# Identity matmul of a key block moved next to its score matmuls in the attention loop of a fused macaron layer

## What is computed

```python
Q = (hidden_states @ Wq.T).reshape(B_, T_, H, D)          # H = 16 heads, D = 128
latent_k = hidden_states @ Wk.T                           # L = 64
latent_v = hidden_states @ Wv.T
q_latent = jnp.einsum('bthd,hdl->bthl', Q, q_to_latent)
logits = jnp.einsum('bthl,bsl->bhts', q_latent, latent_k) * inv_sqrt_L
causal = j <= i
logits = jnp.where(causal[None, None], logits, NEG)
band = (jnp.abs(i - j) <= RA_WINDOW) & causal             # RA_WINDOW = 64
logits = jnp.where(band[None, None], logits + RA_ALPHA * logits_recip, logits)
attn = jax.nn.softmax(logits, axis=-1)
V_exp = jnp.einsum('btl,hld->bthd', latent_v, v_up)
ctx = jnp.einsum('bhts,bshd->bthd', attn, V_exp)
out = ctx.reshape(B_, T_, H * D) @ Wo.T
```

## Time and profile before

| | us |
|---|---|
| median of 3 runs | 3462.59 |
| lowest and highest run | 3459.32, 3469.61 |
| the profiled execution's own time | 3459.25 |
| its span (first to last instruction, slowest core, core 4) | 3457.7 |
| spans of the 8 cores | 3441.6 to 3457.7 |

### The profile page before, as it was taken

How to read it: one execution, slowest core, us unless ns; L and a number is a source line. 1 busy time by engine, 2 the same in 40 slices (tenths; PEclk the granted TensorE clock), 3 DMA queues, 4 the chain that set the end, 5 groups by cost and what they waited for, 6 DMA issues and landing times.

```text
span 3457.7 us, 31678 instructions; the slowest of 8 cores (3441.6 to 3457.7 us)
## 1 busy us (share of the span) xinstructions
PE 2826.7 (82%) x10542; PEld 1005.4 (29%) x10719; DVE 1118.0 (32%) x2081; ACT 696.7 (20%) x1149; POOL 51.4 (1%) x78
## 2 busy tenths in 40 slices
PE   4988669866986698679288888888888888888797
PEld 1333124312432243233022222222222222233333
DVE  2003220332023202411344454555545555411203
ACT  2110211022102210200033333333333333302010
POOL 0000000000000000000000000000000000000000
PEclk8997789888988898889555565565556555689898
DMA  5420233123411341041100000000000000050442
GB/s 134 69 49 0 100 60 65 22 100 49 73 25 73 76 73 25 0 76 34 21 1 1 1 1 1 1 1 1 1 1 1 1 1 1 4 95 0 73 73 98
DMA packets 15218, 128.16 MB, mean 37 GB/s; under 512 B 6417, under 2 KB 6730, under 8 KB 7610
## 3 DMA queue, kind: packets, MB, share of 16 engines
q0 software_dynamic: 6848, 82.28, 14.0%
q1 hardware_dynamic: 8218, 43.83, 3.5%
HBM read 196.53 MB, written 9.27 MB: 60 GB/s over the span
## 4 chain that ended last, share of the span: by engine, by line
PE 76%; DVE 12%; issue 4%; ACT 3%; DMA 3%; DVEq 0%; POOL 0%; ACTq 0%; SPq 0%; POOLq 0%
PE bp_p L318 23%; PE PB L1466 7%; PE PD L1469 7%; PE PC L1390 6%; DVE xhat L242 5%; PE fe_p L573 4%; PE fe_p L515 4%; PE ln_sum L183 4%; PE ln_sum L186 4%; PE PC L1425 3%; PE PA L1255 2%; PE PA L1304 2%; PE bp_p L331 1%; PE bp_cs L288 1%; ACT probs L1447 1%
## 5 line engine op out<-in xcount | busy, mean ns | idle before, releaser
L318 PE MATMUL bp_p<-xhat,wslotP 128*128 128x512 bf16 x2503 | 565.1, 383 | 63.7 <-DVE xhat L242 57.5
L1447 ACT ACTIVATE probs<-PC 128x512 bf16<-128x512 f32 (+3 forms) x768 | 352.7, 486 | 783.6 <-PE PC L1425 483.5
L1466 PE MATMUL PB<-probs,ones_bf 128*1 128x512 bf16 (+3 forms) x768 | 343.4, 447 | 20.2 <-ACT probs L1447 19.3
L318 PEld LDWEIGHTS bp_p<-xhat,wslotP 128*128 128x128 bf16 x2560 | 245.9, 99 | 383.2 <-issue 104.4
L1390 PE MATMUL PC<-qlat_h,kaug 65*128 65x256 bf16 (+3 forms) x1088 | 328.5, 400 | 30.4 <-ACT probs L1447 19.5
L1469 PE MATMUL PD<-probs,vexp 128*128 128x512 bf16 (+3 forms) x705 | 323.9, 459 | 0.0
L176 ACT ACTIVATE ln_sq<-x_res 128x1024 bf16<-128x1024 f32 x144 | 152.1, 1056 | 742.5 <-DVE x_res L583 329.0
L1408 DVE COPY_PREDICATED mr<-bandm_sb,ob 128x256 bf16<-128x256 uint8 (+1 forms) x512 | 210.6, 411 | 111.6 <-DVE ob L1348 63.9
L1425 PE MATMUL PC<-mr,ident_bf 128*128 128x256 bf16 (+1 forms) x576 | 185.2, 343 | 66.0 <-DVE mr L1408 63.5
L358 ACT ACTIVATE bbuf<-bp_p,b_sb 128x1024 bf16<-128x1024 f32 x80 | 89.1, 1114 | 673.7 <-PE bp_p L331 673.7
L242 DVE TENSOR_TENSOR xhat<-x_res,ln_rrep 128x1024 bf16<-128x1024 f32 x144 | 163.6, 1211 | 24.2 <-PE ln_rrep L232 24.2
(11 more groups left out here) (167 smaller groups left out, 2110.4 us busy)
## 6 DMA issues: line engine op xcount, KB each, us to landing
x_res<-xall SPq DMA_DIRECT2D x16, 2048.0 KB, 7.7
wslotP<-w1q POOLq DMA_DIRECT2D x16, 2048.0 KB, 15.1
wslotP<-varr POOLq DMA_DIRECT2D x4, 2048.0 KB, 14.8
wslotP<-uarr POOLq DMA_DIRECT2D x4, 2048.0 KB, 14.8
wslotP<-wqq POOLq DMA_DIRECT2D x4, 2048.0 KB, 15.5
wslotF<-woq POOLq DMA_DIRECT2D x4, 2048.0 KB, 15.7
wslotF<-w1q POOLq DMA_DIRECT2D x4, 2048.0 KB, 15.6
yout<-x_res SPq DMA_DIRECT2D x4, 2048.0 KB
```

The costliest lines, as they stand in the source:

```text
L318: mi = t.matmul(P[par][:, 512 * half:512 * half + 512], lhsT, rhs_sb[:, NTOK * k + 512 * half: NTOK * k + 512 * half + 512], start=(k == 0 ...
L1447: s.activation(probs[i % 2][:, a:b], PC[:, a + dlt:b + dlt], AF.Exp).then_inc(cs.h, 1)
L1466: t.matmul(PB[:, a:b], bufs['ones_bf'][:, 0:1], probs[i % 2][:, a:b], start=(i == 0), stop=last)
```

## The change

Three of the TensorE helpers (scores, imm, sums_ctx) become one, `emit_iter`, which issues in turn `i` sums_ctx of block i-2, scores of block i and then, directly behind them, imm of block i. Before, imm of block i was issued at the head of turn i+1, behind that turn's stage of `emit_A_stage` or epilogue part. exp of block i is now issued at the end of turn i, and so on ScalarE ahead of what the stages and the epilogue of turn i+1 issue; before it stood behind them. outer(i) and select(i) stay where they were on VectorE: behind the turn's stage and epilogue part. No instruction is added or taken away, and no tile, width, DMA or wait condition is changed.

```diff
-                    def emit_scores(i, first_waits):
-                    def emit_imm(i):
-                    def emit_sums_ctx(i):
...
+                    def emit_iter(i, first_waits):
+                        fw = tuple(first_waits)
                         @block.tensor
...
+                            if i >= 2:
+                                j = i - 2
...
+                                for (a, b) in split_ranges(qlo, NTOK, (512,)):
+                                    t.wait_ge(cs.h,
+                                              exp_toks[j][(a + dlt) // 512])
...
+                            if i < NT:
...
+                                    mi = t.matmul(
+                                        PC[:, a + dlt:b + dlt],
+                                        kaug[0:65, 128 * i:128 * i + 128],
+                                        ql[0:65, a:b],
+                                        start=first, stop=stop)
+                                mi.then_inc(ct.h, 1)
+                                sco_toks[i] = ct.inc()
+                            if i < NT:
...
+                                t.wait_ge(cv.h, mr_toks[i])
...
+                                    mi = t.matmul(
+                                        PC[:, a + dlt:b + dlt],
+                                        bufs['ident_bf'][:, :],
+                                        mr_sb[i % 4][:, a - qlo:b - qlo],
+                                        start=False, stop=True)
+                                mi.then_inc(ct.h, 1)
+                                imm_toks[i] = ct.inc()
...
-                        if 1 <= i <= NT:
-                            emit_imm(i - 1)
                         if i < NT:
                             emit_outer(i)
-                        if 1 <= i <= NT:
-                            emit_exp(i - 1)
-                        if i >= 2:
-                            emit_sums_ctx(i - 2)
+                            emit_select(i)
+                        fw = [(dsy.h, st['r64']), PF['pc']] if i == 0 else []
+                        emit_iter(i, fw)
                         if i < NT:
-                            fw = [(dsy.h, st['r64']), PF['pc']] if i == 0 \
-                                else []
-                            emit_scores(i, fw)
-                            emit_select(i)
+                            emit_exp(i)
```

More of the change, by code:

```diff
@@ L1451, in emit_exp, with _ @@
                         exp_toks[i] = toks
-                    def emit_sums_ctx(i):
-                        qlo = qlo_of(i)
+                    def emit_iter(i, first_waits):
+                        fw = tuple(first_waits)
                         @block.tensor
-                        def _(t, i=i, qlo=qlo, st=st, vex=vex,
+                        def _(t, i=i, fw=fw, st=st, vex=vex, ql=ql,
                               pbf=PF['pb'], pdf=PF['pd']):
[L1458 to L1474, removed]
@@ new lines, in _ @@
+                            if i >= 2:
+                                j = i - 2
+                                qlo = qlo_of(j)
+                                dlt = pc_delta(j)
+                                if j == 0:
+                                    t.wait_ge(cv.h, st['ve7'])
+                                    t.wait_ge(pbf[0], pbf[1])
+                                    t.wait_ge(pdf[0], pdf[1])
+                                for (a, b) in split_ranges(qlo, NTOK, (512,)):
+                                    t.wait_ge(cs.h,
+                                              exp_toks[j][(a + dlt) // 512])
+                                    last = (j == NT - 1
+                                            or qlo_of(j + 1) >= b)
+                                    t.matmul(PB[:, a:b],
+                                             bufs['ones_bf'][:, 0:1],
+                                             probs[j % 2][:, a:b],
+                                             start=(j == 0), stop=last)
+                                    mi = t.matmul(
+                                        PD[:, a:b],
+                                        vex[:, 128 * j:128 * j + 128],
+                                        probs[j % 2][:, a:b],
+                                        start=(j == 0), stop=last)
+                                mi.then_inc(ct.h, 1)
+                                sc_toks[j] = ct.inc()
@@ new lines, in _ @@
+                            if i < NT:
+                                qlo = qlo_of(i)
+                                lead = min(256, NTOK - qlo)
+                                dlt = pc_delta(i)
+                                for sem, val in fw:
+                                    t.wait_ge(sem, val)
+                                seen_banks = set()
+                                if dlt == 0:
+                                    pieces = split_ranges(
+                                        qlo, NTOK, (qlo + lead, 512))
+                                else:
+                                    pieces = split_ranges(
+                                        qlo, NTOK, (qlo + lead,))
+                                lead_banks = {(qlo + dlt) // 512,
+                                              (qlo + lead - 1 + dlt) // 512}
+                                pieces.sort(
+                                    key=lambda p: ((p[0] + dlt) // 512
+                                                   in lead_banks, p[0]))
+                                for (a, b) in pieces:
+                                    bank = (a + dlt) // 512
+                                    first = bank not in seen_banks
+                                    if first:
+                                        for back in (1, 2):
+                                            pe = exp_toks.get(i - back)
+                                            if pe is not None and bank in pe:
+                                                t.wait_ge(cs.h, pe[bank])
+                                                break
+                                    seen_banks.add(bank)
+                                    last_in_bank = (b + dlt ==
+                                                    min(512 * (bank + 1),
+                                                        NTOK + dlt))
+                                    stop = (last_in_bank
+                                            and bank not in lead_banks)
+                                    mi = t.matmul(
[5 more added lines that the diff above has]
+                                sco_toks[i] = ct.inc()
@@ new lines, in _ @@
+                            if i < NT:
+                                qlo = qlo_of(i)
+                                lead = min(256, NTOK - qlo)
+                                dlt = pc_delta(i)
+                                t.wait_ge(cv.h, mr_toks[i])
+                                cuts = (512,) if dlt == 0 else ()
+                                for (a, b) in split_ranges(qlo, qlo + lead,
+                                                           cuts):
+                                    mi = t.matmul(
+                                        PC[:, a + dlt:b + dlt],
+                                        bufs['ident_bf'][:, :],
+                                        mr_sb[i % 4][:, a - qlo:b - qlo],
+                                        start=False, stop=True)
+                                mi.then_inc(ct.h, 1)
+                                imm_toks[i] = ct.inc()
```

## The result

The changed kernel takes 3548.32 us (median of 10 runs) against 3461.3 for the kernel before (10 runs): slower by 2.56%, ratio 1.0256 with a 95% interval of 1.0217 to 1.0296. The forecast was 3560 in a range of 3530 to 3595, so time and direction came as predicted. Some executions of every kernel ran with one die's cores at a lower clock; ratios leave them out, and where only two others were left for a variant, both times are given in place of a ratio.

What follows compares the result with a forecast made beforehand. TensorE was taken to set the pace in attention, mostly at 1.2 GHz. Wait terms, chiefly +83.4 us for the loop in turns 26 to 31, summed to +98.7 us on 3459.25, put at 3560 us, range 3530 to 3595.

Steps and rivals of the forecast that it cites:

- TensorE's pace and the closed loop: Attention: TensorE sets the pace; stage matmuls, evacuation, outer, select, imm close a loop of 2.67 or 2.39 us a turn.
- the loop's term: Turns 26 to 31: 14.90 us against 9.48, +5.42; with imm shifts +5.56 a head, +83.4 us over 15 heads.
- Turns 1 and 2: Head start: later rep and stage 0 behind imm(1), +20.0 and +0.5 us; stage 0's long evacuations, +4.5 us.
- Turns 3 to 15: Stages 10 and 11 +3.0 us, stage 12 later +5.0, exponential wait of 0.59 gone -8.9, over 15 heads.
- Turns 22 to 25: Exponential wait of 0.75 us goes, block 24's selection delayed 0.2: -0.55 in 16 heads, -8.8 us.
- The clock: TensorE's granted clock over 15 heads: unknown size, 42 us more to 50 less, taken as 0.
- the sum of 98.7: Whole kernel: all wait terms added, +98.7 us over the kernel before.
- The colder rival: Attention: added waits also take away the 2.4 GHz stretches, 42 us more, 3602 us; chance 0.09.
- the rule of the Trainium skill: TensorE: slow clock is default, recent activity releases it, so added waits cost clock, towards 42 us more.
- The faster rival: Attention: stage matmuls fill TensorE's 34.9 us of waits for exponentials and VectorE keeps up, 3428 us; chance 0.06.

Runs made afterwards that it cites:

- 0.98: Kernel before, with imm and exp of the previous block moved ahead of the stage in turns 4 and 22 alone; ratio 0.9817.
- An edit that removed a wait: Changed kernel with outer and select first in every turn, plus turn 1's epilogue issued behind scores(1) and imm(1); 0.9674, again 0.9727, of the kernel before.

## Why the prediction was right, point by point

- *TensorE's pace and the closed loop.* Shown. The stage matmuls stand 2.62 to 2.65 us apart at 256 columns (forecast 2.67) and 2.37 or 2.38 at 128 (forecast 2.39). Two kinds of distance differ: the last, some 3.05 in the 14 heads with a memset there, and one longer distance in each of three of the 15 heads (2.47, 2.47 and 3.00). The move in these turns alone costs all of the loss, and VectorE's order alone takes it away.
- *The size of the loop's term.* Forecast +5.42 us a head, measured +5.97. The loop as such is 5.29 (14.77 - 9.48, the 14.77 with the memset moved away); the rest, 0.68, is outer(31) beside the memset, which the prediction did not look at, because before the change the two did not meet.
- *Turns 1 and 2.* The forecast of +1.26 to stage 0 came out at +1.23, with the wait of imm(1) at 1.64 where 1.6 was named. rep came 0.4 later behind scores(0) (4.08 in place of 3.66), not 0.5. The two waits of 0.23 and 0.47 us for the selections of blocks 2 and 0 are in the cuts too; the first was forecast as 0.3, the second not.
- *Turns 3 to 15.* The gain at stage 2 was under-sized. The trace gave it as 0.59 us of idle time, but stage 2 to stage 3 became 0.92 shorter (4.93 to 4.01): the matmuls around a wait are stretched too, the sums ahead of it took 2.18 us with the wait and 1.97 without, the scores behind it 0.89 and 0.74. The 0.1 each for stages 10 and 11 did not appear; imm has no wait there.
- *Turns 22 to 25.* Forecast -0.22 with the imm of block 25, measured -0.08. The wait for the exponential is gone and that of turn 24 grew from 0.89 to 1.11, both as said. Not foreseen was 0.22 us before stage 14, where the program has five semaphore waits in a row behind imm. The trace has them from 2393.38 to 2393.89, and imm ends at 2393.73; that they are the cause is likely from this, and no run shows it.
- *The clock.* I took 0, with 50 us less to 42 more as bounds. By idle time the change costs 234 - 129 = 105 us, the sum of 98.7 and the 9.5 of the memset less some; by busy time it gives back 20 us. In the pair of heads above that is 0.87 us between imm(15) and imm(22), where the fast stretch began earlier; on the six cores with complete traces TensorE is busy at 2.4 GHz for 122 us in place of 106 (medians), which makes 16 of the 20. So that 3560 lies so near to 3548 is in part luck: the memset's 9.5 us, which the forecast lacked, and the clock's 16 to 20, which it took as 0, have opposite signs. The colder rival did not come true, and with it the rule of the Trainium skill (TensorE: Matmul & The Clock Gate, Part 1) as I applied it: with 105 us more of idle time the median clock in attention is 0.555 against 0.556, and TensorE's busy time is less, not more.
- *The faster rival* was half there: the waits for exponentials did go, to 0.4. Its price of 35 us was too high by 10, since the trace that it was read from lacks matmuls: 25.2 us on a complete one. The missing matmuls also make the 1011.66 us of busy time in the earlier trace rows too small; core 7, whose trace is complete, is busy for 1032 in as long a stretch. Neither changes the sum, which uses the waits of 0.59 and 0.75 us and not these totals.

## What to carry to other kernels

When work is moved on one in-order queue, look for what stands ahead of its producer on the other queue: imm was moved past a stage on TensorE while the selection still stood behind that stage's evacuation on VectorE, and a pipeline with a turn of slack became a loop. With the producer moved too, the kernel was 4.2% faster than before; of the 146 us in attention 46 are idle time, which the waits let one expect, and 100 are clock, which nothing here let one forecast. Price such a loop from starts to starts in the trace of before; it came out within 0.05 us a turn.

## What was not expected of the hardware

- The clock's part was larger than that of most waits. Between variants with the same instructions TensorE's busy time in attention ranges from 1009 to 1115 us; whole heads run in 82 or 70.4 us in one trace, by the clock of a 31 us stretch (0.98).
- An edit that removed a wait (19 us of idle time) came with 55 us more of busy time, in two pairs of profiles. What decides whether a fast stretch starts was not found.
- TensorE without a gap is no sign of the high clock: the six turns that take 8.30 us are busy for 8.30 us at a granted clock of 0.50, in all 15 heads.
- GpSimd's memset of one row (0.94 us) holds up a `tensor_scalar` of 0.25 us to 0.93 us.
- A wait costs more than its idle figure: 0.92 us for 0.59 in turn 4, and 7.15 for 6.24 over the six turns 26 to 31.
